# Scores as products of 64 columns and true transposes of the keys, in place of one product of both

## The chip, the core and the metric

The kernel runs on one core of a Trainium2 chip. The metric is the device time of one execution in microseconds (us). Five engines work side by side and meet at semaphores: TensorE (PE in the profile, and PEld for its weight loads), VectorE (DVE), ScalarE (ACT), GpSimd (POOL) and SyncE (SP), which issues the DMAs.

## What is computed

A transformer block over x of 8 x 2048 x 256 (16,384 tokens) in float32. Cut to what matters here:

```
h = layernorm(x) * (1 + ca) + sa
q, k, v = h @ Wq, h @ Wk, h @ Wv            # 16 heads of 64; q, k = elu(.) + 1
a = sigmoid(h @ Wa + ba + 2)                # one decay per head and token
S = a_t * S + k_t v_t^T ;  z = a_t * z + k_t          # along the 2048 tokens
out_t = (q_t S) / (q_t z + 1e-6)
x = x + ga * (out @ Wo)
x = x + gb * mixture(layernorm(x) ...)      # 8 experts, 2 chosen per token
```

The recurrence is computed in chunks of 64 tokens: within a chunk a 64 x 64 matrix of scores k^T q, weighted by products of decays; between chunks a state of 64 x 65 (values and a column of ones for z) that needs the keys of the chunk with tokens on the partitions, so transposed.

## The kernel before

Two phases follow each other: attention (`attention_phase`, to about 2575 us of the profile) and the experts (`expert_phase`, the rest). The change is in attention alone.

Attention goes over 32 groups T of 512 tokens (`GT`), 4 groups to a batch row, and in each over 8 pairs u of heads. A *unit* is one pair of heads in one group; there are 256. The work of a unit is spread over four consecutive *steps*, written out by hand for each engine in `attention_steps`: in step (T, u) TensorE does, in this order,

- K and then Q projections of the unit three ahead (`project`, `three_pass`, lines 587 to 589: 6 products of 128x512 each in fp32r, each into its own single bank);
- for the unit one ahead the products of queries and states (line 729, 16 products of 64 x 65), for the unit two ahead the products of keys and values (line 743, 16), and for the unit one ahead the products of weighted scores and values (line 754, 16);
- the transposes of the finished output of this unit (`transpose_o`, line 770, 4 true transposes of 128x128, which in step 0 come after the dense jobs);
- one or two dense jobs from `DENSE_JOBS` (V projection, output projection by Wo, h transposes, the decays' projection `z_job` at line 639);
- last, for the unit three ahead, the block of the change (line 803), here called the *score block*.

All products named with 64 are plain float32 and use a quarter of the array each: 64 rows (one head of the pair, `rows[hd]`) by 64 columns (where the output's partitions lie, `rows[half]`). `place(hd, ch)` says for head hd and chunk ch = 0..7 into which half and which of 4 columns of blocks the result goes: head 0 as the chunks lie, head 1 shifted by one chunk, so that two chunks in a row and both heads use the four quarters of the array.

The score block makes 16 products, one for each chunk and head. The stationary operand is the chunk's keys (64 of head dimension x 64 tokens), the moving one has 128 columns: a unit matrix `eye`, kept in front of q in the tile `qk_sb`, and the chunk's q. So each writes 64 columns of transposed keys (`KTR`) and 64 of scores (`S`) in the two banks `bank_scores`, one bank for each head. The last one increments `s_ps`. In step u the next step's projections follow.

Who waits for `s_ps`: ScalarE copies KTR, scaled by the decays, in 8 activations of 128x64 into `kd_sb` (line 550) and increments `kd_ready`; then VectorE multiplies S by the decays into `p_sb` (line 966, `p_ready`). TensorE needs `kd_ready` at line 743 of the next step, and both before it transposes the output into the bank of scores (line 770). Around them VectorE does per step: k and q's elu (lines 929, 931), the scan of decays (937), the chain of 8 state updates (916) with, in even groups, a clamp ahead of it (903), the row `lam_row` (885, once per group, in step 3), the quotient (951 to 956). ScalarE's order in a step is: relu and exp of K and of Q (510, 512), the output's copies (526, 527), the dense jobs' copies, the 8 of kd.

`ident` is a 128 x 128 unit matrix that the kernel has anyway, for the transposes. `eye8` is VectorE's pattern for the scan.

Of the kernel before, what the change touches and what calls it, by code (L numbers as in the profile page):

```python
# [40 lines left out]
CH = 128  # L41
CK = 64
SLICE = CH // 4
NCH = 4
GT = CH * NCH
NCK = GT // CK
# [98 lines left out]
def attention_phase(nc, tokens, Wq, Wk, Wv, Wo, Wa, ba, c, wmod, x1_dram, gates_dram, rows_dram, mod, ident, bank):  # L145
    with ExitStack() as ctx:
        def sb(name, shape, dt=F32):
            return ctx.enter_context(nc.sbuf_tensor(name, shape, dt))

        def sem(name):  # L150
            return ctx.enter_context(nc.semaphore(name))
# [11 lines left out]
        eye8 = sb("eye8", [128, NCK, CK])  # L163
# [9 lines left out]
        x_res = sb("x_res", [128, NCH, D])  # L173
# [18 lines left out]
        oT_lo = sb("oT_lo", [128, PT, GT], F32R)  # L192
        oT32 = sb("oT32", [128, GT])

        qk_sb = sb("qk_sb", [128, CK + 2 * GT])
        eye, q_sb, k_sb = qk_sb[:, 0:CK], qk_sb[:, CK:CK + GT], qk_sb[:, CK + GT:CK + 2 * GT]
        qs_sb = sb("qs_sb", [128, 2, GT])
        decay = sb("decay", [128, 2, NCH, CK])
        p_sb = sb("p_sb", [128, 2, 2, NCH, CK])
# [12 lines left out]
        Q, K, SCORES, EXTRA, NUM = bank[0][:, :], bank[1][:, :], *bank[2:]  # L212
        U_ODD, U_EVEN = EXTRA[:, 0, :], EXTRA[:, 1, :]
        KTR, S = SCORES[:, :, 0:GT // 2], SCORES[:, :, GT // 2:GT]
        HT = [K, SCORES[:, 1, :]]
        MODS, GATES = SCORES[:, 0, :], NUM[:, 0, :]
        KTR_S = SCORES[:, :, :].rearrange("p h (x t i) -> p h x t i", x=2, t=NCH)
        U = [(U_EVEN, U_ODD)[ch % 2][:, ch // 2 * VW:(ch // 2 + 1) * VW] for ch in range(NCK)]
        def o_bank(u):

# [6 lines left out]
        consts_ready = sem("consts_ready"); carry_ready = sem("carry_ready"); ones_ready = sem("ones_ready"); fills = sem("fills")  # L227
# [14 lines left out]
        decay_ready = sem("decay_ready"); qs_ready = sem("qs_ready")  # L242
        s_ps = sem("s_ps"); p_ready = sem("p_ready")
        kd_ready = sem("kd_ready")
        u_ps = sem("u_ps"); eye_ready = sem("eye_ready"); entry_clamped = sem("entry_clamped"); state_step = sem("state_step")
        inter_ps = sem("inter_ps"); num_ps = sem("num_ps"); den_step = sem("den_step"); o_ready = sem("o_ready")
        oT_ps = sem("oT_ps"); oT32_ready = sem("oT32_ready"); oT_hi_ready = sem("oT_hi_ready"); oT_lo_ready = sem("oT_lo_ready")

# [1 line left out]
        def wide(t, dims):  # L250
            return t.rearrange(f"p {dims} -> p ({dims})")

        v_flat = wide(v_sb[:, :, :, :], "c h v")
        p_flat = wide(p_sb[:, :, :, :, :], "a h t i")
        qk_flat, qs_flat, res_flat = qk_sb[:, CK:CK + 2 * GT], wide(qs_sb[:, :, :], "a n"), wide(x_res[:, :, :], "c d")
        wmod_part = [[p_flat[:, 0:3 * D], qk_flat[:, 0:3 * D]], [qs_flat[:, 0:3 * D], res_flat[:, 0:3 * D]]]
        W = KT * P_DIM
        WQ, WV, WK, WO0, WO1 = range(5)
# [16 lines left out]
        def place(hd, ch):  # L275

            m = (ch - hd) % NCK
            return m % 2, m // 2
# [98 lines left out]
        def _(pool):  # L377
# [31 lines left out]
            for t, fill, pattern in ((eye8[:, :, :], 1.0, [[0, NCK], [-1, CK]]), (first[:, :], 1.0, [[-1, 1]]), (later[:, :], 0.0, [[-1, 1]])):  # L409
                pool.affine_select(out=t, in_=t, compare_op=ALU.not_equal, fill=fill, base=-CK, pattern=pattern,  # L410
                                   channel_multiplier=1).then_inc(consts_ready, 1)
            pool.wait_ge(consts_ready, 6)
            pool.tensor_copy(eye, eye8[:, 0, :]).then_inc(eye_ready, 1)
            reciprocal_deviation(0)
            ln_apply(0, range(NCH))
            pool.memset(carry[:, :, :, :], 0.0).then_inc(carry_ready, 1)
# [141 lines left out]
        def _(pe):  # L558
# [3 lines left out]
            for kt in range(KT):  # L562
                mm = pe.transpose(K[:, kt * BATCH:(kt + 1) * BATCH], c_e[:, kt * 128:(kt + 1) * 128],
                                  ident[0:BATCH, 0:BATCH])
# [3 lines left out]
            for m, sec in enumerate(SECTION):  # L568
                for kt in range(KT):
                    col = (m * KT + kt) * BATCH  # L570
                    cols = slice((sec % 3) * D + kt * 128, (sec % 3) * D + (kt + 1) * 128)
                    for k2 in range(KT):
                        pe.matmul(MODS[:, col:col + BATCH], wmod_part[sec // 3][k2][:, cols], silu_t[:, k2, :],
                                  start=(k2 == 0), stop=(k2 == KT - 1))
            for g in range(2):
                for k2 in range(KT):
                    mm = pe.matmul(GATES[0:BATCH, g * D:(g + 1) * D], silu_t[:, k2, :],
                                   wmod_part[g][k2][:, 2 * D:3 * D], start=(k2 == 0), stop=(k2 == KT - 1))
# [121 lines left out]
            def step(T, s, u):  # L700
                n = T * PAIRS + u
                Tc, pc, c = unit(T, u, 1)
                Tb, pb, b = unit(T, u, 2)
                Ta, pa, a = unit(T, u, 3)
                sa = s if u + 3 < PAIRS else 1 - s
                sc = s if u + 1 < PAIRS else 1 - s
                rows = [slice(i * CK, (i + 1) * CK) for i in range(2)]
# [11 lines left out]
                if exists(Tc):  # L719
# [5 lines left out]
                    for ch in range(NCK):  # L725
                        state = carry[:, sc, pc, :] if ch == 0 else s_mid[:, pc % 2, ch - 1, :]
                        query = slice(ch * CK, (ch + 1) * CK)
                        for hd in range(2):
                            mm = pe.matmul(NUM[rows[ch % 2], hd, ch // 2 * VW:(ch // 2 + 1) * VW], qs_sb[rows[hd], pc % 2, query],
                                           state[rows[hd], :], start=(ch < 2), stop=False)  # L730
                    mm.then_inc(inter_ps, 1)
                if exists(Tb):
# [7 lines left out]
                    for ch in range(NCK):  # L740
                        for hd in range(2):
                            half, t = place(hd, ch)
                            mm = pe.matmul(U[ch][rows[hd], :], kd_sb[rows[half], t, rows[hd]], v_sb[rows[half], t, v_col(pb, hd), :],
                                           start=True, stop=True)
# [41 lines left out]
                if exists(Ta):  # L786

                    pe.wait_ge(k_ready, a + 1)
                    pe.wait_ge(q_ready, a + 1)
                    after(pe, kd_ready, a)  # L790
                    after(pe, p_ready, a)
                    if u and exists(T):
                        pe.wait_ge(oT_hi_ready, n + 1)
                    if u == 0 and exists(T + 1):
                        pe.wait_ge(h32_ready, T * 2 + 4)
                    if isinstance(Ta, int) and a == 0:
                        pe.wait_ge(eye_ready, 1)
                    pe.sem_inc(inputs_seen)
                    for ch in range(NCK):
                        eye_q = qk_sb[:, 0:2 * (ch + 1) * CK].rearrange("p (x i) -> p x i", x=2)[:, :, 0:CK]  # L800
                        for hd in range(2):
                            half, t = place(hd, ch)
                            mm = pe.matmul(KTR_S[rows[half], hd, :, t, :], k_sb[rows[hd], ch * CK:(ch + 1) * CK], eye_q[rows[hd], :, :],  # L803
                                           start=True, stop=True)
                    mm.then_inc(s_ps, 1)

            attention_steps(pe, step)
# [636 lines left out]
```

## Time and profile before

| | us |
|---|---|
| median of 3 runs | 3454.72 |
| the three runs | 3454.70, 3454.72, 3460.96 |
| the profiled execution, its own time | 3456.77 |
| its span in the profile | 3455.0 |
| TensorE busy (matmuls) | 3259.2 (94%) |
| VectorE busy | 2604.3 (75%) |
| ScalarE busy | 1816.2 (53%) |
| GpSimd busy | 1425.9 (41%) |

A row of a group of instructions names line, engine, operation, output <- inputs (for a product: moving operand, then stationary), the part of the array used as rows*columns, the shape, the count, and then busy time and the mean duration of one. Matmuls overlap: the mean duration of one is far above the distance from one start to the next. A row of the timeline gives the start, the time from the first start to the last end, and what ran; consecutive instructions of one line are merged into one row with their count. Each float32 product appears as two matmuls and two weight loads; a true transpose and an fp32r product appear as one of each.

### The profile page before, as it was taken

Reading aid. Unit: us, or ns where it says so; the run is one execution under the profiler, and the core shown is the slowest. Engines: PE = TensorE matmul, PEld = TensorE weight load, DVE = VectorE, ACT = ScalarE, POOL = GpSimd, SP = SyncE. Lnnn points to the kernel's source line nnn. Section 1 sums busy time; section 2 is a strip of 40 time slices with the busy share of each in tenths; the row PEclk is TensorE's granted clock in tenths of the full one; section 3 lists DMA queues with packets and bytes.
Section 4 is the critical chain, followed back from the end, with each engine's and each line's share of the span. In section 5 each row is a group of like instructions: output and inputs, shape, how many; then the busy total and the mean of one; then the engine's idle time right before and its main releaser. Section 6 shows DMA issues by size and latency. Waiting matters only on the chain. (4 is left out here: it accounts for less than half of the span.)

```text
span 3455.0 us, 130112 instructions
## 1 busy us (share of the span) xinstructions
PE 3259.2 (94%) x51114; PEld 2754.8 (80%) x51114; DVE 2604.3 (75%) x6738; ACT 1816.2 (53%) x4493; POOL 1425.9 (41%) x1122
## 2 busy tenths in 40 slices
PE   6999999999999999999999999999986999999999
PEld 5888888888887887888888888888875777777777
DVE  5777877777777877787777778787755788778786
ACT  4666666666666665666666666666632222322321
POOL 4444444545444444445454444444431222222222
PEclk9999999999999999999999999999987999999999
DMA  4222222222222222222222322222212111111110
GB/s 139 76 76 74 74 82 71 80 72 73 81 87 77 74 77 72 75 73 78 75 73 77 92 74 73 77 77 76 70 42 80 44 44 38 50 38 38 46 41 25
DMA packets 158635, 238.79 MB, mean 69 GB/s; under 512 B 30232, under 2 KB 82504, under 8 KB 157768
## 3 DMA queue, kind: packets, MB, share of 16 engines
q1 hardware_dynamic: 158024, 230.33, 21.1%
q8 instruction: 421, 6.90, 0.8%
q14 instruction: 190, 1.56, 0.2%
HBM read 194.58 MB, written 35.67 MB: 67 GB/s over the span
## 5 line engine op out<-in xcount | busy, mean ns | idle before, releaser
L447 POOL TENSOR_TENSOR qs_sb<-lam_bc,qk_sb 128x512 f32<-128x512 f32 x256 | 521.7, 2038 | 1150.3 <-DVE qk_sb L931 976.8
L550 ACT ACTIVATE kd_sb<-bank_scores,decay 128x64 f32<-128x64 f32 x2048 | 448.0, 330 | 290.3 <-PE bank_scores L803 283.4
L916 DVE SCALAR_TENSOR_TENSOR s_mid<-s_mid,lam_bc,bank_dense 128x65 f32<-128x65 f32 x1536 | 433.3, 282 | 55.9 <-DVE s_mid L916 1.3
L455 POOL TENSOR_TENSOR oT_lo<-oT,oT_hi 128x512 fp32r<-128x512 f32 x256 | 328.4, 1283 | 84.1 <-ACT oT_hi L527 83.8
L510 ACT ACTIVATE qk_sb<-bank 128x512 f32<-128x512 f32 x512 | 316.7, 619 | 70.7 <-PE bank L589 56.3
L512 ACT ACTIVATE qk_sb<-qk_sb 128x512 f32<-128x512 f32 x512 | 323.3, 632 | 16.3
L587 PE MATMUL bank<-wv_hi,h_hi 128*128 128x256 f32 x1024 | 307.7, 300 | 24.9 <-DVE qk_sb L929 11.0
L966 DVE TENSOR_TENSOR p_sb<-bank_scores,decay 128x512 f32<-128x512 f32 x256 | 176.1, 688 | 190.5 <-ACT kd_sb L550 188.7
L937 DVE TENSOR_TENSOR_SCAN decay<-a_bc,eye 128x512 f32<-128x512 f32 x256 | 310.9, 1214 | 1.3 <-DMA a_bc<-rows_dram 1.3
L1292 DVE SCALAR_TENSOR_TENSOR acc<-bank,comb,acc 128x256 f32<-128x256 f32 x512 | 229.6, 475 | 103.0 <-ACT acc L1160 93.4
L803 PE MATMUL bank_scores<-qk_sb 64*64 64x128 f32 x8192 | 288.1, 276 | 13.8 <-ACT oT_hi L527 4.3
L682 PE MATMUL bank<-wo_hi,oT_hi 128*128 128x256 f32 x1024 | 289.3, 283 | 1.6 <-DVE xo L841 0.8
L588 PE MATMUL bank<-wv_lo,h_hi 128*128 128x256 f32 x1024 | 287.7, 281 | 1.3 <-issue 1.3
L589 PE MATMUL bank<-wv_hi,h_lo 128*128 128x256 f32 x1024 | 287.3, 281 | 0.0
L683 PE MATMUL bank<-wo_lo,oT_hi 128*128 128x256 f32 x1024 | 286.5, 280 | 0.0
L684 PE MATMUL bank<-wo_hi,oT_lo 128*128 128x256 f32 x1024 | 286.5, 280 | 0.0
L803 PEld LDWEIGHTS bank_scores<-qk_sb 64*64 64x64 f32 x8192 | 226.7, 133 | 54.8 <-issue 40.2
L1292 DVE SCALAR_TENSOR_TENSOR acc<-bank_scores,comb,acc 128x256 f32<-128x256 f32 x512 | 230.8, 476 | 50.4 <-PE bank_scores L1206 47.8
L931 DVE SCALAR_TENSOR_TENSOR qk_sb<-bank,qk_sb 128x512 f32<-128x512 f32 x256 | 176.5, 690 | 114.5 <-ACT qk_sb L512 113.4
L526 ACT ACTIVATE oT<-bank_scores 128x512 f32<-128x512 f32 x224 | 134.0, 598 | 240.8 <-PE bank_scores L770 239.3
L1120 POOL TENSOR_TENSOR acc<-acc,gb 128x512 f32<-128x512 f32 x64 | 82.9, 1296 | 427.8 <-DVE acc L1292 409.6
L587 PE MATMUL bank<-h_hi,wk_hi 128*128 128x512 f32 x512 | 229.5, 448 | 16.8 <-ACT oT_hi L527 10.0
(204 smaller groups left out, 8795.9 us busy)
## 6 DMA issues: line engine op xcount, KB each, us to landing
a_bc<-rows_dram SPq DMA_DIRECT2D x512, 128.0 KB, 3.1
lam_bc<-rows_dram SPq DMA_DIRECT2D x512, 128.0 KB
x_in<-in_L_attn_x_dram SPq DMA_DIRECT2D x32, 512.0 KB, 5.0
x_res<-in_L_attn_x_dram SPq DMA_DIRECT2D x32, 512.0 KB, 3.9
x_dram<-x_res SPq DMA_DIRECT2D x32, 512.0 KB, 2.9
x<-x_dram SPq DMA_DIRECT2D x32, 512.0 KB, 3.3
out_dram<-x SPq DMA_DIRECT2D x32, 512.0 KB, 2.9
ew_raw<-in_L_ffn_expert_W_dram SPq DMA_DIRECT2D x8, 256.0 KB, 5.7
```

The source lines that it names most:

```text
L447: pool.tensor_tensor(qs_sb[:, na, :], lam_bc[na][:, :], q_sb, ALU.mult).then_inc(qs_ready, 1)
L455: pool.tensor_tensor(oT_lo[:, u, :], oT32[:, :], oT_hi[:, u, :].bitcast(F32), ALU.subtract).then_inc(oT_lo_ready, 1)
L510: act.activation(t, x[:, :], ACT.Relu, scale=-1.0).then_inc(x_neg, 1)
L512: act.activation(t, t, ACT.Exp, scale=-1.0).then_inc(x_exp, 1)
L550: ins = act.activation(kd_sb[:, t, hd * DH:(hd + 1) * DH], KTR[:, hd, t * CK:(t + 1) * CK], ACT.Copy, scale=decay[:, hd, t, CK - 1:CK])
L587: pe.matmul(dst, s_hi, m_hi, start=(n == 0), stop=False)
L588: pe.matmul(dst, s_hi, m_lo, start=False, stop=False)
L682: pe.matmul(dst, oT_hi[:, pt, tok], wo_hi[:, pt, :], start=(pt == 0 and i == 0), stop=False)
L803: mm = pe.matmul(KTR_S[rows[half], hd, :, t, :], k_sb[rows[hd], ch * CK:(ch + 1) * CK], eye_q[rows[hd], :, :], start=True, stop=True)
L916: dve.scalar_tensor_tensor(dst, src, lam_bc[nb][:, (ch + 1) * CK - 1:(ch + 1) * CK], U[ch], ALU.mult, ALU.add).then_inc(state_step, 1)
L937: dve.tensor_tensor_scan(decay[:, :, :, :].rearrange("p h t i -> p (h t i)"), a_bc[na][:, :], eye8[:, :, :].rearrange("p c i -> p (c i)"), ...
L1292: dve.scalar_tensor_tensor(a, y[:, (k // 2) * D:(k // 2 + 1) * D], comb[s % 2][:, 2 * pair + i, e:e + 1], a, ALU.mult, ALU.add).then_inc(y ...
```

## The change

Each product of 128 moving columns becomes one of 64, for the scores alone. The transposed keys come from `pe.transpose` of 64 rows (one head) by 128 tokens (two chunks at once), 4 for head 0 and 3 for head 1; the two chunks of head 1 that the shift leaves alone at the ends (7 and 0) are made by plain products with the unit matrix. All of it stands before the same increment of `s_ps`. `eye`, its copy at the start and its semaphore go; `qk_sb` gets 64 columns shorter.

```diff
-        qk_sb = sb("qk_sb", [128, CK + 2 * GT])
-        eye, q_sb, k_sb = qk_sb[:, 0:CK], qk_sb[:, CK:CK + GT], qk_sb[:, CK + GT:CK + 2 * GT]
+        qk_sb = sb("qk_sb", [128, 2 * GT])
+        q_sb, k_sb = qk_sb[:, 0:GT], qk_sb[:, GT:2 * GT]
...
-        KTR_S = SCORES[:, :, :].rearrange("p h (x t i) -> p h x t i", x=2, t=NCH)
...
-            pool.wait_ge(consts_ready, 6)
-            pool.tensor_copy(eye, eye8[:, 0, :]).then_inc(eye_ready, 1)
...
-                    if isinstance(Ta, int) and a == 0:
-                        pe.wait_ge(eye_ready, 1)
                     pe.sem_inc(inputs_seen)
                     for ch in range(NCK):
-                        eye_q = qk_sb[:, 0:2 * (ch + 1) * CK].rearrange("p (x i) -> p x i", x=2)[:, :, 0:CK]
+                        tok = slice(ch * CK, (ch + 1) * CK)
                         for hd in range(2):
                             half, t = place(hd, ch)
-                            mm = pe.matmul(KTR_S[rows[half], hd, :, t, :], k_sb[rows[hd], ch * CK:(ch + 1) * CK], eye_q[rows[hd], :, :],
-                                           start=True, stop=True)
+                            pe.matmul(S[rows[half], hd, t * CK:(t + 1) * CK], k_sb[rows[hd], tok], q_sb[rows[hd], tok], start=True, stop=True)
+                    for ch in (NCK - 1, 0):
+                        half, t = place(1, ch)
+                        pe.matmul(KTR[rows[half], 1, t * CK:(t + 1) * CK], k_sb[rows[1], ch * CK:(ch + 1) * CK], ident[rows[1], rows[1]],
+                                  start=True, stop=True)
+                    for t in range(NCH):
+                        for hd in range(2 if t < NCH - 1 else 1):
+                            mm = pe.transpose(KTR[:, hd, t * CK:(t + 1) * CK], k_sb[rows[hd], t * CH + hd * CK:(t + 1) * CH + hd * CK],
+                                              ident[rows[hd], rows[hd]])
                     mm.then_inc(s_ps, 1)
```

## Rows read from the trace of the kernel before

**Rows 1.** The page: busy time by engine; busy tenths and clock by slice.
```profile
span 3455.0 us, 130112 instructions
PE 3259.2 (94%) x51114; PEld 2754.8 (80%) x51114; DVE 2604.3 (75%) x6738; ACT 1816.2 (53%) x4493; POOL 1425.9 (41%) x1122
...
PE   6999999999999999999999999999986999999999
...
PEclk9999999999999999999999999999987999999999
```

**Rows 2.** An even group, an odd one, a light step: length, busy times, clock.
```profile
1005.47:1086.77 81.30, 76.26 (x1425) 64.96 (x1421) 62.78 (x143) 49.62 (x128) 37.77 (x27) 1.00 0.25 75
1086.77:1163.40 76.63, 75.12 (x1425) 64.77 (x1421) 58.09 (x139) 49.70 (x128) 37.77 (x27) 1.00 0.25 78
1142.13:1149.83 7.70, 7.66 (x161) 6.43 (x157) 7.23 (x19) 5.79 (x15) 3.36 (x3) 1.00 0.23 70
```

**Rows 3.** Timeline of TensorE around one score block.
```profile
1202.97 0.60 PE L649 MATMUL bank<-ident,a_cols 128*80 128x128 f32 x4
1203.50 1.10 PE L803 MATMUL bank_scores<-qk_sb 64*64 64x128 f32 x32
1204.53 0.50 PE L587 MATMUL bank<-h_hi,wk_hi 128*128 128x512 f32 x1
1204.87 0.39 PE L588 MATMUL bank<-h_lo,wk_hi 128*128 128x512 f32 x1
1205.11 0.39 PE L589 MATMUL bank<-h_hi,wk_lo 128*128 128x512 f32 x1
```

**Rows 4.** Timeline of TensorE from one block of 64-column products to full-array ones.
```profile
1209.06 0.68 PE L743 MATMUL bank_dense<-v_sb,kd_sb 64*64 64x65 f32 x32
1209.53 0.68 PE L754 MATMUL bank_nums<-v_sb,p_sb 64*64 64x65 f32 x32
1210.13 0.66 PE L770 MATMUL bank_scores<-ident,o_sb 128*128 128x128 f32 x4
1210.55 0.36 PE L587 MATMUL bank<-wv_hi,h_hi 128*128 128x256 f32 x1
```

**Rows 5.** Timeline of TensorE into a block that uses 128*32 of the array.
```profile
1115.12 0.28 PE L588 MATMUL bank<-wv_lo,h_hi 128*128 128x256 f32 x1
1115.24 0.28 PE L589 MATMUL bank<-wv_hi,h_lo 128*128 128x256 f32 x1
1115.44 0.74 PE L639 MATMUL bank<-wa,h 128*32 128x16 f32 x64
```

**Rows 6.** TensorE groups by shape: busy us, mean ns, idle before.
```profile
L803 PE MATMUL bank_scores<-qk_sb 64*64 64x128 f32 x8192 | 288.1, 276 | 13.8 <-ACT oT_hi L527 4.3 <-issue 4.1 <-ACT h L490 0.2
L754 PE MATMUL bank_nums<-v_sb,p_sb 64*64 64x65 f32 x8192 | 178.1, 220 | 22.2 <-issue 22.0 <-PE bank_nums L729 0.2
L770 PE MATMUL bank_scores<-ident,o_sb 128*128 128x128 f32 x896 | 149.3, 290 | 1.4 <-DVE o_sb L956 1.4
```

**Rows 7.** TensorE waits from 130 to 2480 us: total, times, longest.
```profile
PE bank L587 <- DVE lam_row L885: 26.3, 25, 1.8
PE bank_nums L754 <- issue: 18.5, 11, 2.5
PE bank L587 <- DVE qk_sb L929: 9.6, 14, 0.9
PE bank_nums L729 <- issue: 9.3, 31, 0.4
PE bank L587 <- ACT oT_hi L527: 8.6, 30, 0.3
```

**Rows 8.** Timeline of a light step: work behind the score block.
```profile
1142.31 1.75 ACT L550 ACTIVATE kd_sb<-bank_scores,decay 128x64 f32<-128x64 f32 x8 [0.61 <-PE bank_scores L803]
1143.90 0.65 ACT L510 ACTIVATE qk_sb<-bank 128x512 f32<-128x512 f32 x1
1144.16 0.69 DVE L966 TENSOR_TENSOR p_sb<-bank_scores,decay 128x512 f32<-128x512 f32 x1
...
1145.64 0.67 PE L743 MATMUL bank_dense<-v_sb,kd_sb 64*64 64x65 f32 x32
```

**Rows 9.** Step 0 of two groups; then a stretch of the first.
```profile
1324.34:1338.84 14.50, 14.27 (x201) 12.44 (x201) 7.27 (x16) 6.43 (x13) 5.24 (x6) 0.88 0.08 29
1244.54:1257.62 13.08, 12.79 (x204) 11.50 (x201) 7.01 (x16) 8.11 (x21) 6.54 (x7) 1.00 0.08 23
1325.61:1329.02 3.41, 3.41 (x20) 2.30 (x22) 0.69 (x1) 1.38 (x3) 0.00 (x0) 0.50 0.01 2
```

**Rows 10.** Timeline: the idle time of TensorE ahead of that step 0.
```profile
1324.34 0.50 PE L587 MATMUL bank<-h_hi,wk_hi 128*128 128x512 f32 x1 [3.33 <-issue]
```

More of the change, by code:

```diff
@@ L244, in attention_phase @@
         kd_ready = sem("kd_ready")
-        u_ps = sem("u_ps"); eye_ready = sem("eye_ready"); entry_clamped = sem("entry_clamped"); state_step = sem("state_step")
+        u_ps = sem("u_ps"); entry_clamped = sem("entry_clamped"); state_step = sem("state_step")
         inter_ps = sem("inter_ps"); num_ps = sem("num_ps"); den_step = sem("den_step"); o_ready = sem("o_ready")
@@ L254, in attention_phase @@
         p_flat = wide(p_sb[:, :, :, :, :], "a h t i")
-        qk_flat, qs_flat, res_flat = qk_sb[:, CK:CK + 2 * GT], wide(qs_sb[:, :, :], "a n"), wide(x_res[:, :, :], "c d")
+        qk_flat, qs_flat, res_flat = qk_sb[:, 0:2 * GT], wide(qs_sb[:, :, :], "a n"), wide(x_res[:, :, :], "c d")
         wmod_part = [[p_flat[:, 0:3 * D], qk_flat[:, 0:3 * D]], [qs_flat[:, 0:3 * D], res_flat[:, 0:3 * D]]]
```

## Prediction
> **What bounds the kernel now.** I read the page first: TensorE is busy 94% of the span, the slices show 9 tenths or more all through attention, and the clock is granted in full nearly everywhere [rows 1]. The next busiest engine has 75%. So attention is bound by TensorE's stream, and what the score block costs on TensorE is what counts. Then the stretches by group: an odd group takes 76.63 us with TensorE busy 75.12, an even one 81.30 with 76.26; the even one has 4.7 us more of VectorE work (62.78 against 58.09) and is 4.7 us longer [rows 2]. There TensorE waits for VectorE in places, so not every nanosecond added to or taken from TensorE reaches the end. Then the waits of TensorE, to count those places [rows 7], and last the timeline around the blocks of 64-row products [rows 3 to 5], from which the new block is put together.
>
> **How the array is paid.** The score block runs from 1203.50 to the next block's first start at 1204.53, 1.03 us [rows 3]. It has 32 matmul records. The block of line 754 has 32 as well, with 65 columns in place of 128. Two such blocks follow each other at 1209.06 and 1209.53: 0.47 us for 32, 58.8 ns for four [rows 4], though one record lasts 220 ns on average [rows 6]. So four quarters of the array run side by side, and each takes a new matmul every 58.8 ns. When the block ends and the full array is used next, it takes 0.60 us (1209.53 to 1210.13) in place of 0.47: 0.13 us are lost where the shape of the array in use changes [rows 4]. The same is seen where only the columns change: from the 128*128 product at 1115.24 to the 128*32 one at 1115.44 it takes 0.20 us, where two products of that kind lie 0.12 apart [rows 5], 0.08 lost. With that the score block reads as 1.03 - 0.13 = 0.90 us for 8 rounds of four, about 0.05 of it the first weight load, which nothing covers, so (0.90 - 0.05) / 8 = 106 ns a round of 128 columns. The split is rough by 0.02. The four true transposes of 128x128 take 1210.13 to 1210.55, 0.42 us for four, of which the first weight load is again about 0.05; so a fp32 transpose of 128 moving columns takes about 0.09 to 0.11 us [rows 4], the same as one round of 128 columns. A transpose is one record where a product is two.
>
> **The change part by part, TensorE's time per unit.**
> - The 16 products of 64 columns: 8 rounds of four at the rate of the 65-column blocks, 8 x 58 = 464 ns in place of 8 x 106 = 850. Saves 386 ns.
> - The two plain products of head 1: 4 records, but both use the same 64 rows and differ only in the column half, so two quarters work and two rounds are needed: 2 x 58 = 116 ns. Between 58 (if they slip in beside other quarters) and 4 x 58 = 232 (one after another).
> - 7 true transposes of 64 rows x 128 tokens. No row of before shows this shape. Their moving operand has 64 columns, so half of a 128-column transpose: about 58 ns for one. Each uses 64 rows and all columns, so two lie side by side, head 0 four and head 1 three; head 0 decides: 4 x 58 = 230 ns. Bounds: 7 x 30 = 210 if every pair overlaps perfectly, 7 x 105 = 735 if each costs as much as the 128x128 one and none overlap. I take 230, since it follows the row nearest to it, the quarters running side by side in line 754.
> - One more change of the array's shape, from 64*64 to 64*128, in the middle of the block. Loss between 0 (the row group stays as it is, nothing to drain) and 0.15 (0.13 of rows 4 with more weights to load, uncovered). I take the loss between 64*64 and 128*128, which is 0.13 less the part that the exposed load has, 0.09, and 0.055 for the first load of 128 columns: 145 ns. Rows 5 show that a change of columns alone is enough for such a loss.
> - The change of shape to the next projection was there before; it stays.
>
> Sum: -386 + 116 + 230 + 145 = +105 ns. The rows are rounded to 10 ns, and the sum is a small difference of large terms, so I count it the other way too: the new block has 8 + 2 + 4 = 14 short rounds in place of 8 long ones. If a long round is twice 53 ns of streaming and the same 4 ns on top that a short one has (58.8 for 65 columns), it is 110 in place of 106, and 14 x 58 - 8 x 110 + 145 = +77. I take +75 ns per unit, and as bounds -90 (no loss at the change of shape) and +260 (the transposes one after another).
>
> The Trainium skill, "TensorEngine Tiling (Array Packing)", Key Properties, says that changing the tiling mode, not merely the tile, drains TensorE. Rows 4 and 5 agree with it (0.13 and 0.08 us at such changes); by it the loss of the fourth item is certain, and the sum stays positive. The same page, Restrictions, says that column tiling excludes transposes of fp32 input, which is why the changed shape can't be avoided by transposing in quarters; no row here tests that.
>
> **What of it reaches the end.** 256 units, so 19 us if all of it did. But TensorE waits at some places behind a score block for something that does not depend on it, and there a longer block only shortens the wait: 30 times for ScalarE's copy of the output before the next group's second step, 25 times for `lam_row`, 31 times ahead of line 729, 14 times for k in the dense jobs [rows 7], together 100 of the 256. A part of the other steps of even groups is bound by VectorE too (rows 2: their extra length equals VectorE's extra work). I count 150 of 256 as reaching the end: 150 x 0.075 = +11 us; between 100 (+7) and 256 (+19).
>
> **What is behind the increment.** The increment still sits on the last instruction, and ScalarE's 8 copies of kd start as long after the end of the block as before. Their chain is: kd done at 1144.06, p written at 1144.85, the products that need kd at 1145.64 [rows 8]. That leaves 1.6 us for kd; the block's growth moves both sides alike. So no new wait there. The instruction count grows by 11 matmuls and 11 weight loads per unit; the stops in which TensorE waits for nothing visible, 18.5 us in 11 stops at line 754 [rows 7], may get a little more or fewer; I price it at 0 with +-3 us. The removed copy on GpSimd and the wait for it are of the start, where TensorE waits for weights anyway: 0; if that cover were gone it would be under 1 us, once. The dropped 64 columns of `qk_sb` move nothing. The experts' phase is the same code: 0.
>
> **Sum.** Profiled execution 3456.77 us (span 3455.0), 2 us above the median of 3454.72. Forecast for the median: 3454.7 + 11 = 3466 us, its own range 3457 to 3476.
>
> **Rivals.**
> - *The transposes don't overlap* (two row halves with all columns wait for each other, or for each other's weight load). Head 1's three then add 3 x 58 = 172 ns, the block +75 + 172 = +247 ns. For a longer block fewer waits absorb it: some 190 units, +47 us: 3502. For: no row shows two such tiles together, and every true transpose in the trace uses the whole array. Against: all quarters of 64 rows do run side by side.
> - *No loss at the new change of shape* (the other side, faster). The rows in use stay in two halves of 64, and a weight load could go ahead into a free half. Then the block is 75 - 145 = -70, at best -90 ns: -11 to -14 us over the same 150 units: 3443. It decides as soon as the loss is below some 70 ns. For: the change is only in the columns. Against: rows 5.
> - *The clock.* In one group's step 0 the granted clock was 0.88 on average, with 3.4 us at 0.50, which is 1.2 GHz, and the step took 14.50 us in place of 13.08 [rows 9]: 1.4 us for one such dip. Ahead of that step TensorE had stood idle for 3.33 us [rows 10]. If TensorE with many short transposes were taken for less busy, dips would come more often; one more in every second group would be 16 x 1.4 = +22, with the 11 above 3488. Against: 4 full transposes per step are there now at full clock [rows 1, 6], and the new ones are 0.2 to 0.4 us of a step of 8 to 13 us. The Trainium skill, "TensorE: Matmul & The Clock Gate", Part 4, says that work in transpose mode does not count as a busy TensorE in the same way; that speaks for this rival.
> - *VectorE hides all of it*: the steps of even groups and the light ones (7.70 us, of which VectorE works 7.23 [rows 2]) would absorb the block's growth: 3455 to 3460.
>
> **How the numbers follow.** Forecast 0.47; not overlapping 0.20; no loss 0.17; clock 0.07; hidden by VectorE 0.09. What a measurement here can tell from no change is about 0.2%, 7 us: under 3447.8 faster, above 3461.6 slower. Of the forecast's 0.47 some 0.35 lie above it and 0.12 within. Slower 0.35 + 0.20 + 0.07 = 0.62; faster 0.14 of the third case and 0.02 of others; same the rest, 0.22. The range goes from the case without loss, 3441, to the transposes one after another, 3504.
>
> **What would show it.** In the changed kernel's timeline: the score products of 64x64 should take about 0.5 us for 32 records; between the last plain product and the first transpose some 0.15 us; the 7 transposes start in pairs a few ns apart, the pairs 58 ns apart. The block from its first product to the next projection should take 1.03 + 0.075 = 1.10 us; 0.95 says no loss, 1.28 no overlap. An odd group should grow from 76.6 by about 0.4 us and an even one by less. Wrong would be the prediction if the block grew and the groups did not, or the granted clock fell below its present share of the slices.

## The result: 3460.86 us, 0.18% slower, and the profile after

| | before | after |
|---|---|---|
| median of 20 executions each, us | 3454.71 | 3460.86 |
| ratio, 95% interval | | 1.0018 (1.0011 to 1.0025) |
| profiled execution: own time, span | 3456.77, 3455.0 | 3463.85, 3462.1 |

One execution of each kernel (3965 and 4561 us), and one of plain below (4462 us), ran far above all others; the ratios and plain's row in the table leave them out, and the medians above hardly move by them.

The page of the changed kernel, to be laid beside [rows 1]. It has 2816 more matmuls, 11 for each of 256 units, 9.7 us more TensorE busy time in a span 7.1 us longer, and 441 instruction fetches where before had 421.
```profile
span 3462.1 us, 135742 instructions
PE 3268.9 (94%) x53930; PEld 2778.6 (80%) x53930; DVE 2605.0 (75%) x6738; ACT 1815.2 (52%) x4493; POOL 1423.9 (41%) x1121
...
PEclk9999999999999999999999999999987999999999
...
q8 instruction: 441, 7.23, 0.9%
```

Timeline of TensorE around one score block of the changed kernel, the counterpart of [rows 3]. Line 798 are the score products, 801 the two plain ones, 805 the seven transposes.
```profile
1155.44 0.69 PE L798 MATMUL bank_scores<-qk_sb 64*64 64x64 f32 x32
1155.96 0.29 PE L801 MATMUL bank_scores<-ident,qk_sb 64*64 64x64 f32 x4
1156.18 0.46 PE L805 MATMUL bank_scores<-ident,qk_sb 64*128 64x64 f32 x7
1156.57 0.50 PE L584 MATMUL bank<-h_hi,wk_hi 128*128 128x512 f32 x1
1156.91 0.40 PE L585 MATMUL bank<-h_lo,wk_hi 128*128 128x512 f32 x1
```
Read by the distances between starts: 0.52 + 0.22 + 0.39 = 1.13 us, against 1.03 in [rows 3]. Over all the blocks of the trace the medians are 1.134 and 1.034: +0.100 us per unit, 25.6 us over 256 units. A quarter of it is in the result.

An even group and the odd one after it, the counterpart of [rows 2] (length, then busy us of PE, PEld, DVE, ACT, POOL, the granted clock):
```profile
1012.38:1092.87 80.49, 76.61 (x1511) 65.83 (x1508) 62.81 (x143) 49.58 (x128) 37.79 (x28) 1.00 0.24 75
1092.87:1170.17 77.30, 75.98 (x1511) 65.98 (x1508) 58.14 (x139) 49.88 (x128) 37.26 (x28) 1.00 0.26 77
```
The odd group is 0.7 us longer, close to the 0.8 that 8 longer blocks add. The even one, in which VectorE does 4.7 us more, is not longer at all (80.49 against 81.30). The medians over all groups point the same way: odd 76.63 to 77.71, even 80.91 to 80.49. The odd ones grew by more than 0.8: TensorE's idle time in them grew as well (24.5 to 28.8 us over the 14 odd groups from 2 to 29). In the even ones it shrank (64.0 to 58.6 us), and so did the time at half clock (30.7 to 3.0 us), of which the odd ones had next to none in either kernel.

TensorE's waits in the changed kernel, 130 to 2480 us, the counterpart of [rows 7] (us, times, longest):
```profile
PE bank L584 <- DVE lam_row L887: 26.3, 29, 1.7
PE bank_nums L751 <- issue: 12.9, 9, 2.2
PE bank L585 <- issue: 10.2, 8, 1.9
PE bank_scores L798 <- issue: 7.3, 14, 1.3
PE bank L584 <- DVE qk_sb L931: 7.0, 9, 0.9
...
PE bank L584 <- ACT oT_hi L524: 5.5, 28, 0.2
```
The wait for the output's copy shrank from 8.6 to 5.5 us and the one for k from 9.6 to 7.0: longer blocks eat waits. The sum for `lam_row` stayed, but its longest fell from 1.8 to 1.7, which matters below. The stops where TensorE waits for nothing visible ("issue") are at other lines: 18.5 us at the line-754 block went to 12.9, and 10.2 us came up in the middle of projections. All of them together came to 42.0 us before and 45.0 after.

### The profile page after: what moved, and what is told of

Same layout as the page of the kernel before. It is cut to its first block and busy times, and to the rows that moved or that the text cites. A ratio compares the mean times of both kernels' runs of the same rounds, so it can differ in the third digit from the quotient of the medians.

```text
span 3462.1 us, 135742 instructions
## 1 busy us (share of the span) xinstructions
PE 3268.9 (94%) x53930; PEld 2778.6 (80%) x53930; DVE 2605.0 (75%) x6738; ACT 1815.2 (52%) x4493; POOL 1423.9 (41%) x1121
## 5 line engine op out<-in xcount | busy, mean ns | idle before, releaser
L585 PE MATMUL bank<-wv_lo,h_hi 128*128 128x256 f32 x1024 | 287.5, 281 | 10.2 <-issue 10.2
L933 DVE SCALAR_TENSOR_TENSOR qk_sb<-bank,qk_sb 128x512 f32<-128x512 f32 x256 | 176.6, 690 | 111.4 <-ACT qk_sb L509 109.0
L584 PE MATMUL bank<-h_hi,wq_hi 128*128 128x512 f32 x512 | 206.2, 403 | 30.2 <-DVE lam_row L887 29.0
L931 DVE SCALAR_TENSOR_TENSOR qk_sb<-bank,qk_sb 128x512 f32<-128x512 f32 x256 | 175.5, 686 | 56.5 <-ACT qk_sb L509 55.5
```

The source lines that it names most:

```text
L584: pe.matmul(dst, s_hi, m_hi, start=(n == 0), stop=False)
L585: pe.matmul(dst, s_hi, m_lo, start=False, stop=False)
```

## The experiments

Each ran beside new executions of the kernel before, on one chip. "Block" is the median distance from the block's first matmul to the next projection, from the trace. The time over the base is the difference of the medians. Two further numbers come from each trace, both from 20 us after the first K projection to 5 us ahead of the last: the sum of the gaps between matmul records ("idle", good to about 1 us), and the time at half clock (granted clock 0.50). The names that begin with b_ are changes of the kernel before, those with a_ the same changes of the changed kernel.

| kernel | block, us | growth x units, us | time over its base, us | idle, us | half clock, us |
|---|---|---|---|---|---|
| before | 1.034 | | | 103.6 | 34.1 |
| the change | 1.134 | 25.6 | +6.2 | 99.9 | 6.8 |
| pad1 | 1.253 | 56 | +26.5 | 82.3 | 13.7 |
| pad4 | 1.471 | 112 | +43.4 | 58.7 | 3.4 |
| plain | 1.092 | 15 | +8.1 | 99.8 | 20.5 |
| split | 1.418 | 98 | +40.0 | 62.2 | 10.2 |
| turn | 1.134 | 25.6 | +6.9 | 93.6 | 6.8 |
| only | 0.742 | -65 | -29.2 | 131.7 | 41.0 |
| b_noclamp | 1.034 | | | 54.0 | 6.8 |
| a_noclamp, over b_noclamp | 1.134 | 25.6 | +15.8 | 42.1 | 3.4 |
| b_static | 1.034 | | | 122.0 | 23.9 |
| a_static, over b_static | 1.134 | 25.6 | +13.2 | 110.6 | 13.7 |
| b_shift | 1.034 | | | 96.7 | 27.3 |
| a_shift, over b_shift | 1.134 | 25.6 | +19.6 | 94.4 | 13.7 |

### A longer block without the change: pad1 and pad4

```diff
-                    for ch in range(NCK):
+                    for ch in [*range(NCK), 7]:            # pad1; pad4: 4, 5, 6, 7
```


> The kernel before with the two products of chunk 7 (128 columns) issued a second time in every score block: one more round of four, 109 ns per unit, 27.9 us over 256 units, with only 4 matmuls and 4 weight loads more. It lengthens the block about as much as the change did (+0.10 us) without its instructions, its shapes or its new change of shape. Theory A (part of any longer score block is hidden by waits of TensorE that shrink, and the rest was given back by fewer stretches at half clock): +5 to +12 us, ratio 1.0015 to 1.0035. Rival B (the change was cheap because of something in it, and the block's growth as such arrives in full): +20 to +28 us.

> The kernel before with the products of chunks 4 to 7 issued a second time: four more rounds, 436 ns per unit, 112 us over 256 units. Theory A (waits hide a growth only up to their length, 0.3 to 1.8 us each, and only in about 100 of 256 steps): the slope gets steeper with the dose, +65 to +85 us. Rival B (all arrives): +105 to +112. Rival C (VectorE bounds most steps): under +50.

Measured: pad1 1.0084 (1.0071 to 1.0097), pad4 1.0123 (1.0108 to 1.0138). The block of pad1 grew by 219 ns and not by 109: repeated at once, chunk 7's two products find only their own two quarters of the array, busy with the first copy, and take two rounds. So the growth was 56 us, and 47% of it arrived; of pad4's 112 us, 39%. For pad1 neither figure set beforehand applies, since the dose was twice the intended one: +26.5 lies in the range of rival B, but B said that all of the growth arrives. pad4's +43.4 is a miss for theory A, which had set +65 to +85, and lies in the range of rival C (VectorE bounds most steps, under +50). Neither "all arrives" nor "only the waits' length is hidden, so the slope steepens" holds: between the doses 56 us more cost 17 us more. The table shows where it went: TensorE's idle time fell from 103.6 to 82.3 and 58.7 us, and time at half clock from 34.1 to 13.7 and 3.4. Nor is it the even groups alone that absorb it. With 1.75 and 3.5 us more in each group (groups 2 to 29), the median odd group grew by 1.0 and 1.8 us, the even one by 0.6 and 1.1. So TensorE alone does not set the pace in the odd groups either.

### Parts of the block: plain, split, turn

plain (the keys by 16 plain products, in place of the 9 instructions of the change):
```diff
-                    for ch in (NCK - 1, 0):
-                        ...
-                    for t in range(NCH):
-                        ...
+                    for ch in range(NCK):
+                        for hd in range(2):
+                            half, t = place(hd, ch)
+                            mm = pe.matmul(KTR[rows[half], hd, t * CK:(t + 1) * CK], k_sb[rows[hd], ch * CK:(ch + 1) * CK],
+                                           ident[rows[hd], rows[hd]], start=True, stop=True)
```


> The changed kernel with the 9 instructions for the keys replaced by 16 plain products of 64 columns with the unit matrix: no new shape of the array in the block. TensorE's arithmetic for the block: 16 short rounds of 58 ns and one first load of 51 and one drain of 150, 1.12 us, against 1.13 measured in the changed kernel and 1.03 before; 64 matmul records per unit in place of 43 and 32. Theory A: time within 5 us of the changed kernel, +4 to +12 over before. Rival D (the stops for instructions grow with their number): 10 us or more above the changed kernel.

Measured: 1.0022 (1.0013 to 1.0031), block 1.092 us. The 32 additional records take 8 rounds, 0.61 us, with no change of shape; the change's two plain products and seven transposes take 0.61 as well (0.22 + 0.39). The transposes save nothing; the whole block, 1.092 against 1.134 us, is even shorter with plain products, though the end is not (+8.1 against +6.2, the same within the noise). 485 fetches in place of 441 did not cost 10 us either, so the number of instructions as such is not what counts.

split (two changes of shape more: four transposes, the two plain products, three transposes):
```diff
+                    for part in (keys_t[:4], keys_t[4:]):
+                        for t, hd in part:
+                            mm = pe.transpose(...)
+                        if part[0] == (0, 0):
+                            ...                              # the two plain products
```


> The changed kernel with the two plain products moved between the fourth and the fifth transpose: two more changes of the array's shape in every block, nothing else added. If a change of shape costs what the trace of the changed kernel shows (149 ns between starts in place of some 50, and a first load): the block grows by 0.25 to 0.30 us, and the end by +40 to +70 us over the changed kernel. Rival: the gap in the trace is waiting for something else (the semaphore or the queue) and splitting costs under 0.1 us a block, +10 us or less.

Its timeline (802 transposes, 807 plain products):
```profile
1163.60 0.34 PE L802 MATMUL bank_scores<-ident,qk_sb 64*128 64x64 f32 x4
1163.87 0.33 PE L807 MATMUL bank_scores<-ident,qk_sb 64*64 64x64 f32 x4
1164.13 0.34 PE L802 MATMUL bank_scores<-ident,qk_sb 64*128 64x64 f32 x3
1164.39 0.50 PE L584 MATMUL bank<-h_hi,wk_hi 128*128 128x512 f32 x1
```
Measured: 1.0114 (1.0099 to 1.0128), the block +0.284 us over the changed kernel with not a matmul more: 0.14 us for each change of shape, as the prediction had it. The end grew by 33 us, under the +40 to +70 that had been set: of the 73 us that the blocks grew by, 45% arrived.

turn (all transposes of head 0 first):
```diff
-                    for t in range(NCH):
-                        for hd in range(2 if t < NCH - 1 else 1):
+                    for hd in range(2):
+                        for t in range(NCH - hd):
```


> The changed kernel with the order of the 7 transposes turned: all four of head 0, then the three of head 1, in place of alternating. If the two row halves run side by side when they alternate, the block grows by 3 x 58 = 0.17 us, and the end by +20 to +45 us over the changed kernel. If they don't overlap as it is, the block and the end stay (within 3 us).

```profile
1155.19 0.46 PE L805 MATMUL bank_scores<-ident,qk_sb 64*128 64x64 f32 x7
1155.58 0.50 PE L584 MATMUL bank<-h_hi,wk_hi 128*128 128x512 f32 x1
```
Measured: 1.0023 (1.0013 to 1.0032), block unchanged (0.39 us for the seven, as before the turn). By the letter this is the outcome set for "they don't overlap". The single records say otherwise: in both kernels the transposes start in pairs, 3 ns apart in the changed kernel and 13 ns in turn; the second pair starts 111 ns after the first, the next ones 60 to 65 ns apart. They overlap in both; turning the order did not separate them (see the last section). The experiment did not test what it was made for.

### How much of TensorE's time counts: only

The transposes and one plain product left out in groups 2 to 29.
```diff
-                    for ch in (NCK - 1, 0):
+                    for ch in (NCK - 1, 0) if isinstance(T, int) else (NCK - 1,):
...
-                    for t in range(NCH):
+                    for t in range(NCH if isinstance(T, int) else 0):
```


> The changed kernel with the transposes and one of the two plain products left out in the loop (groups 2 to 29; the keys' transposed copy is not computed there, ScalarE copies what lies in the bank). The block becomes 0.51 + 0.06 + 0.15 = 0.72 us in place of 1.03 before: TensorE saves 0.31 us per unit, 224 units, 70 us. Theory A with VectorE close behind TensorE: only a part arrives, -15 to -40 us against before. If TensorE alone bounded the steps: -60 to -70 us.

Measured: 0.9916 (0.9903 to 0.9929), -29 us of 65: 45%. Idle rose by 28 us and half clock by 7. The share is that of pad1 in the other direction, so it is no effect of added work; the range set for a partial arrival held, "TensorE alone bounds the steps" did not.

### VectorE's part: the kernels without the clamp

```diff
-                if sb_ == 0 and not (isinstance(Tb, int) and Tb == 0):
+                if False and sb_ == 0 and not (isinstance(Tb, int) and Tb == 0):
```


> The kernel before without VectorE's clamp of the entry state (1.2 us, 8 times in every second group; the state's reset between batch rows is left out). If VectorE bounds the even groups: they fall from 80.9 to about 76.8 us, -55 to -65 us in all. If TensorE does: no change.

> The changed kernel without the clamp (the reset is left out). Theory A' (the change's +0.10 us per unit is hidden where VectorE is late, that is in the even groups): without the clamp the change costs about as much in even groups as in odd ones, +1.1 us a group or more, so this kernel is +20 to +30 us above the kernel before without its clamp. Rival (hidden elsewhere, by the clock or the waits for the copies and lam_row, which stay): +5 to +12 us as with the clamp.

An even and an odd group of the kernel before without the clamp, then of the changed kernel without it:
```profile
979.63:1055.67 76.04, 75.00 (x1424) 64.59 (x1420) 55.79 (x137) 49.75 (x128) 38.49 (x27) 1.00 0.27 80
1055.67:1131.77 76.10, 75.07 (x1424) 64.69 (x1421) 55.73 (x137) 49.70 (x128) 38.47 (x27) 1.00 0.27 80
```
```profile
989.18:1065.80 76.62, 75.75 (x1512) 65.82 (x1509) 55.85 (x137) 49.71 (x128) 38.47 (x28) 1.00 0.24 79
1065.80:1142.88 77.08, 76.15 (x1511) 66.08 (x1508) 55.86 (x137) 49.89 (x128) 37.99 (x28) 1.00 0.26 79
```
Measured: b_noclamp 0.9779 (0.9766 to 0.9791), -74.7 us, more than the -55 to -65 set; a_noclamp 0.983 (0.9817 to 0.9843), 15.8 us above it. The 4.7 us by which even groups are longer come with VectorE's clamp: the groups are alike without it. Part of them is the clock: TensorE's wait for `lam_row`, up to 1.8 us with the clamp, is 0.8 at most without it, and the time at half clock fell from 34.1 to 6.8 us. And without the clamp the change costs the same in even and odd groups (medians 76.20 and 76.21 become 76.67 and 76.68) and 62% of the 25.6 us arrives. The figure set was 20 to 30, the rival's 5 to 12; 15.8 lies between, so VectorE's lateness by the clamp is not all that hides the longer block.

### The clamp at a fixed address: b_static and a_static

```diff
+                    if pb == 0:
+                        dve.tensor_scalar(limit[:, :], widest[:, :], bound[:, bass.ds(i, 1)], neg_bound[:, bass.ds(i, 1)],
+                                          ALU.min, ALU.max).then_inc(limit_set, 1)
+                        dve.wait_ge(limit_set, i)
-                    dve.tensor_scalar(entry, entry, bound[:, bass.ds(i, 1)], neg_bound[:, bass.ds(i, 1)], ...)
+                    dve.tensor_scalar(entry, entry, limit[:, 0:1], limit[:, 1:2], ...)
```


> The kernel before with the clamp's two bounds taken once per even group into a tile at a fixed address, so that the 8 clamps of the group read fixed addresses (the trace of before has 120 clamps, median 1217 ns, shortest 293 ns, in groups whose number the program knows beforehand). Nothing is left out. If the 0.92 us per clamp are the price of the address from a register, VectorE saves 8 x 0.92 - 1.3 = 6 us per even group and, VectorE being what binds there, the kernel gains most of what it gained without the clamp (75 us): -45 to -70 us, about 3395. Rival (the price is in the two pointer scalars or in min and max): no change.

> The changed kernel with the same fixed-address clamp. By theory A' (VectorE's lateness in even groups hides part of the longer block) the change costs here about what it cost without any clamp (15.8 us by medians), +12 to +20 us above b_static, and not the 6 us that it cost with the slow clamp.

VectorE's groups in b_static (busy us, mean ns):
```profile
L912 DVE TENSOR_SCALAR carry<-carry,limit 128x65 f32<-128x65 f32 x120 | 146.7, 1222 | 0.5
L909 DVE TENSOR_SCALAR limit<-widest,bound,neg_bound 128x2 f32<-128x2 f32 x15 | 17.8, 1186 | 0.0
```
Measured: b_static 1.005 (1.0037 to 1.0064), a miss. The clamp costs 1222 ns with its bounds at a fixed address too, and the same instruction on 2 columns, with bounds addressed by a register, costs 1186: the price is in this form of instruction, not in the address or the 65 columns. Whether it is the two bounds read from memory or min and max was not tried. (One clamp of 120 in the trace of before took 293 ns, two in that of the changed kernel were as short, none in b_static was, and nothing here explains it.) The 15 additional instructions lengthen one step of every odd group by 1.48 us (median 13.577 to 15.058, the step in which the next group's first entry is clamped), 22 us in all, which is more than the whole loss of 18: there 1.19 us of VectorE's time arrives at more than its own length. a_static came 13.2 us above b_static, inside the 12 to 20 forecast, but the reason given (a fast clamp) did not come about; it stands as one more measurement of the change's cost, in another program.

### The place of the instructions: b_shift and a_shift

```diff
-            for kt in range(KT):
+            for kt in [*range(KT)] * 33:
                 mm = pe.transpose(K[:, kt * BATCH:(kt + 1) * BATCH], c_e[:, kt * 128:(kt + 1) * 128], ...)
```


> The kernel before with TensorE's first two transposes (of the conditioning vector, before the weights are there) issued 33 times over: 64 matmuls and 64 weight loads more at the start, so that every later instruction of TensorE lies 128 instructions further on against the fetches of some 16 KB (6.90 MB in 421 fetches). The start grows by up to 8 us (64 x 0.1), hidden as far as TensorE waits there for weights. If the stops inside blocks (34.5 us of idle time in the trace of before) hang on where the fetches fall, they move to other lines and their sum changes by 5 to 15 us; if they hang on the data or on semaphores they stay at the same lines.

> The changed kernel with the same 128 instructions at the start. Same two readings. If the stops' place sets part of the change's cost, the difference to b_shift is not the 6 us between the two kernels, but anything from 0 to 15.

Measured: b_shift 0.9996 (0.9985 to 1.0007), a_shift 1.005 (1.0036 to 1.0064); by medians the change costs 19.6 us here. The first K projection comes 3.8 us later in both. In the kernel before three stops inside the block of line 754, each with its successor one turn of the loop later (some 1107 to 1111 us):
```profile
285.04 0.34 PE L754 MATMUL bank_nums<-v_sb,p_sb 64*64 64x65 f32 x6 [1.52 <-issue]
1391.99 0.34 PE L754 MATMUL bank_nums<-v_sb,p_sb 64*64 64x65 f32 x6 [1.81 <-issue]
650.93 0.34 PE L754 MATMUL bank_nums<-v_sb,p_sb 64*64 64x65 f32 x7 [1.18 <-issue]
1759.84 0.34 PE L754 MATMUL bank_nums<-v_sb,p_sb 64*64 64x65 f32 x7 [0.92 <-issue]
1200.75 0.39 PE L754 MATMUL bank_nums<-v_sb,p_sb 64*64 64x65 f32 x10 [1.89 <-issue]
2312.23 0.39 PE L754 MATMUL bank_nums<-v_sb,p_sb 64*64 64x65 f32 x10 [2.15 <-issue]
```
The count is what is left of the 32 matmuls: the stop falls at the same instruction in both turns. The same holds for ten of the eleven such stops above 0.4 us in the loop's first turn, wherever they lie. In b_shift the waits read:
```profile
PE bank_scores L770 <- issue: 8.2, 5, 2.4
...
PE bank_nums L754 <- issue: 5.8, 4, 2.1
```
18.5 us at line 754 became 5.8, and 8.2 came up at line 770. The sum of the gaps inside blocks fell from 34.5 to 13.8 us, more than the 5 to 15 set; in the changed kernel it went from 31.9 to 28.3. So the stops hang on where an instruction lies in the program, as the first reading had it. But most of what left the blocks came back between them: counting the stops at a block's first instruction too, all of this kind went from 42.0 to 38.4 us, and in the changed kernel from 45.0 to 37.7. The difference a_shift minus b_shift, 19.6, lies outside the "0 to 15" set for it, and the stops don't explain it: in all they differ by 0.7 us between these two kernels, by 3.0 between the two without the shift.

## Why the prediction was right in size and where its steps were off

**What bounds.** Right in part. That VectorE's clamp lengthens the even groups is shown by the noclamp pair. That the odd groups are TensorE's alone is not so: only about half of what pad1 and pad4 added to them arrived, and without the clamp, where all groups are alike, 62% of the change's growth did.

**The block.** Forecast +75 ns (bounds -90 to +260), measured +100; the first of the two sums had given +105. (The upper bound took the price of a lone transpose as 58 ns; with the prediction's own 7 x 105 = 735 ns it would have been +610.) The parts, start to start. The saving on the scores: from first to last start 835 ns before, 477 after, 358 in place of 386; the rest of the saving is in the last round's end, the fourth part. The plain products and the change of shape behind them: 266 ns from the last score product to the first transpose, two rounds and one drain as forecast (116 + 150). The transposes: 237 ns from first to last and 154 to the next projection, the latter 45 less than before, where a round of 128 columns had to run out. With -358 + 266 + 237 - 45 = +100 the sum closes. The terms are those of the prediction; the saving was taken at the favourable end (a long round at 110 ns, where it is (835 - 51 - 20) / 7 = 109, with 51 ns for the first weight load and 20 between the first and the last start of a round, and short rounds of transposes at 58, where they are 60 to 65). Of the rivals, "no loss at the change of shape" is refuted by split, and "the transposes don't overlap" by the records in pairs: seven of them take 237 ns from first start to last. The pairs were to be 58 ns apart; the second comes 111 ns after the first. The Trainium skill's rule that a change of tiling mode drains TensorE ("TensorEngine Tiling (Array Packing)", Key Properties) agrees with split: 0.14 us each.

**How much reaches the end.** The step with the largest error. The prediction took 150 of 256 units, +11 us, and 100 at the least. At the forecast's own share the measured block would give +15, at its least share +10. It came to +6.2 (3.8 to 8.6 by the interval), and to +15.8, +13.2 and +19.6 in the three other pairs of kernels that differ by the change alone (4 to 11 executions each, so rough by 4 to 5 us). So 60 units in one program and 160, 130 and 200 in others: the share is no property of the change. The time of 3461 lay inside the forecast's own 3457 to 3476, but by luck in part: the block came out longer than forecast, the share smaller, and the two errors were of opposite sign. Counted out, the lowest share gives 3462; only the margin that the range had below it took in the 3461. The signs set for the groups show it: an odd group was to grow by 0.4 us and grew by 1.1, an even one by less and shrank.

**What was missing.** Two terms. First the clock: the prediction's rival had it fall, and it rose. In the trace 34.1 us of attention ran at half clock before and 6.8 after, worth 13.6 us of work. It is not one execution's luck: the mean granted clock was 0.9846 in 33 executions of the kernel before and 0.9878 in 19 of the changed one, and 0.0032 x 3455 = 11 us is an estimate of what that gave back. With it the profiled pair closes: 25.6 us of longer blocks, less 13.6, less 3.7 of idle time that shrank, is 8.3, against 9.0 between the first and last K projection. This is bookkeeping, which says where the time went and not why. The same sum gives 24.5 against 22.8 for pad1, 45 against 39 for split, -34 against -31 for only, 12.0 against 12.0 for the noclamp pair; it is rougher for pad4 (52 against 45), plain (4 against 9) and shift (17 against 24).

The traces show what TensorE did before the clock fell. Before, each of the ten stretches at half clock began with the end of a stop or within 1.3 us of it: four times a stop for nothing visible, of 1.88 to 3.33 us, and six times the wait for `lam_row`, of 1.83 or 1.84 us. One such wait in the kernel before and the stretch behind it at a granted clock of 0.50, then one in another even group of the changed kernel, where it stayed at 1.00:
```profile
577.38 0.48 PE L587 MATMUL bank<-h_hi,wq_hi 128*128 128x512 f32 x1 [1.84 <-DVE lam_row L885]
578.10:581.50 3.40, 3.40 (x72) 2.56 (x75) 2.24 (x5) 1.23 (x2) 0.00 (x0) 0.50 0.24 59
1056.02 0.47 PE L584 MATMUL bank<-h_hi,wq_hi 128*128 128x512 f32 x1 [1.74 <-DVE lam_row L887]
1056.02:1059.50 3.48, 3.48 (x105) 2.87 (x106) 2.93 (x7) 1.23 (x2) 0.00 (x0) 1.00 0.32 94
```
This wait shrinks by as much as the block ahead of it grows: with blocks longer by 0.058, 0.100, 0.219, 0.384 and 0.437 us (plain, the change, pad1, split, pad4) it is 1.77, 1.74, 1.61, 1.44 and 1.39 us in place of 1.83, and 2.12 in only, where the block is 0.29 shorter.

In the three traces with the old block and the clamp (before, b_static, b_shift) 14 of the 28 waits of 1.82 to 1.84 us were followed by a stretch at half clock; in the four with the new block and the clamp (the change, turn, a_static, a_shift) none of the 34 waits of 1.71 to 1.75 us was. In only 6 of 13 were followed by one; in plain, pad1, split and pad4 none was. (Beside these, most kernels have one longer wait near the end of attention, 1.80 to 2.2 us; it was followed by such a stretch in six kernels and not in the change and turn.) In the noclamp pair the wait is at most 0.8 us and the mean clock was 0.9882 in both, so the change had nothing to win there. No run changed this wait alone, so what it does to the clock is read from traces and not isolated.

Idle time as a sum does not do as the cause: b_static had more of it than before and a higher mean clock (0.9858), b_shift less of it and the same clock (0.9845). With the clock's part added back as above (11, 0, 4 and 10 us) the change costs 17, 16, 17 and 30 us in its four pairs. So the clock accounts for most of the spread of three of them, and why the shifted pair costs more stays open.

The Trainium skill's remark on transpose mode ("TensorE: Matmul & The Clock Gate", Part 4) would have had the clock fall. plain, without the transposes, had the same mean clock as the changed kernel, 0.9879, so no run here shows transposes counting for less.

Second the stops for nothing visible, priced at 0 with 3 us either way. In the profiled pair they grew by 3.0 us in all (42.0 to 45.0), at the edge of that. But their place is a matter of the placement of the code, and with it went more than they account for: the same change cost 6.2 us at one placement and 19.6 at another.

**The rest.** The increment's place, the copies behind it, the start and the experts' phase (from the last K projection to the end 901.0 us before, 899.2 after) did nothing that needs a term.

## What to carry to other kernels

Price a block by start-to-start rounds, and count a change of the array's shape in the middle of it (0.14 us here) as you would count work. Where two engines run close, multiply TensorE's gain or loss by a share measured in both directions (here 39 to 47% for doses of 56 to 112 us and -65), don't expect it to hold for a small one (the change's own 25.6 us arrived at 24 to 77%), and look for the second engine's one costly instruction first: leaving out one clamp was worth 75 us, the whole dispute over the block 6. Look too at what a longer or shorter block does to the longest waits: here 0.1 us less of one wait went with 27 us less at half clock. Differences below some 15 us in a program of long unrolled loops should be tried at two placements of the code before they are called a property of the change.

## What the runs showed of the hardware that was not expected

- **Matmuls of different row halves did not start in program order.** In turn, head 0's four transposes stand ahead of head 1's three, and the last one carries the increment. In its trace the record with the increment starts 204 ns before the next projection and a record without it 154 ns before. The Trainium skill ("TensorE: Matmul & The Clock Gate", Part 3) says that matmuls start and end in program order; these records differ. ScalarE's first copy came 182 ns after the projection's start, 157 in the changed kernel, so the increment may still have waited for the last one.
- **A clamp of 128x65 with two bounds per partition took as long as one of 128x2** (1222 and 1186 ns), against 282 for the state update on the same 65 columns.
- **Stops of 0.9 to 2.5 us repeat at the same instruction in each turn of a loop**, and moved when 128 instructions were put ahead of everything; their sum moved by 3.6 and 7.3 us.
- **Waits of 1.82 to 1.84 us were followed by 3.4 us at half clock in 14 of 28 cases, waits of 1.71 to 1.75 us in none of 34**, in traces of the same phase.
